# A first stage that interleaves the layer-0 product, the projection weights and the first tile's projections

## What is computed

```python
x = x + x @ w_eff.T                      # layer 0: w_eff from a codebook of 64 levels
...
q, k, v = x @ Wq.T, x @ Wk.T, x @ Wv.T   # layer 1: 32 query heads, 8 key heads, D = 128
q, k = rope(rmsnorm(q)), rope(rmsnorm(k))
k_all = concat(k_cache[block_table], k)  # 512 cached keys + 32 new ones per batch
probs = softmax(where(valid, q @ k_all.T * SCALE, -1e30))
x = x + (probs @ v_all) @ Wo.T
```

## Time and profile before

| | us |
|---|---|
| median of 3 runs | 2267.26 |
| lowest, highest | 2263.91, 2267.69 |
| profiled execution | 2268.09 |
| its span, first to last instruction | 2266.1 |

### The profile page before, as it was taken

How to read it: one execution, slowest core, us unless ns; L and a number is a source line. 1 busy time by engine, 2 the same in 40 slices (tenths; PEclk the granted TensorE clock), 3 DMA queues, 4 the chain that set the end, 5 groups by cost and what they waited for, 6 DMA issues and landing times.

```text
span 2266.1 us, 61278 instructions
## 1 busy us (share of the span) xinstructions
PE 2165.7 (96%) x18068; PEld 1417.1 (63%) x18068; DVE 1728.6 (76%) x3942; ACT 1470.7 (65%) x4967; POOL 1242.9 (55%) x2067
## 2 busy tenths in 40 slices
PE   5786779999999999999999999999999999999998
PEld 2343456666666666666666666666666666666665
DVE  6996458777787777777777777777777777777785
ACT  2542267777776767776667767777666666666674
POOL 3421026656655665555666666665665656656663
PEclk9997889999999999999999999999999999999999
DMA  3784666667667666666768768666666666566663
GB/s 102 225 282 165 216 221 202 191 204 204 195 195 216 204 199 205 204 197 198 208 186 259 207 184 253 176 176 179 190 180 178 176 180 188 177 178 177 183 180 99
DMA packets 472535, 438.32 MB, mean 193 GB/s; under 512 B 52861, under 2 KB 399308, under 8 KB 471694
## 3 DMA queue, kind: packets, MB, share of 16 engines
q1 hardware_dynamic: 427086, 295.96, 44.1%
q0 software_dynamic: 40960, 134.25, 19.3%
q10 hardware_dynamic: 4160, 4.19, 0.5%
HBM read 377.50 MB, written 56.70 MB: 192 GB/s over the span
## 4 chain that ended last, share of the span: by engine, by line
PE 83%; DVE 1%; issue 0%; ACT 0%; another core or an unknown queue 0%; DVEq 0%; ACTq 0%
PE PR L1058 21%; PE Op L1037 15%; PE WOp L1095 15%; PE Sp L1003 14%; PE PTp L1014 11%; PE TRp L1071 3%; PE Sp L1006 2%; PE Op L1019 1%; PE Op L1039 1%; PE TRp L1082 1%; DVE masked L1280 0%; DVE pts L1285 0%; DVE OT L1298 0%; DVE y L1335 0%; DVE masked L1291 0%
## 5 line engine op out<-in xcount | busy, mean ns | idle before, releaser
L778 POOL DMA_INDIRECT pages<-values_split,rows x512 | 516.0, 1008 | 194.4 <-issue 181.4
L1058 PE MATMUL PR<-Wt,xT 128*128 128x512 f16 x2304 | 557.0, 380 | 1.9 <-DVE Wt L1343 1.9
L1166 ACT ACTIVATE pts<-PTp 128x512 f16<-128x512 f32 x512 | 305.9, 597 | 357.9 <-PE PTp L1014 278.8
L1037 PEld LDWEIGHTS Op<-pts,pages 128*128 128x128 f16 x6144 | 384.9, 98 | 126.0 <-DVE OT L1298 8.1
L1037 PE MATMUL Op<-pts,pages 128*128 128x128 f16 x6144 | 426.7, 219 | 6.1 <-DVE OT L1298 5.2
L1280 DVE CUSTOM_DVE_ANT_0 masked<-Sp,mask 128x544 f32<-128x544 f32 x512 | 369.7, 722 | 81.9 <-PE Sp L1006 41.0
L1003 PE MATMUL Sp<-pages,qT 128*128 128x512 f16 x1536 | 415.7, 379 | 3.5 <-PEq L184 3.4
L1172 ACT ACTIVATE masked<-masked,small 128x544 f32<-128x544 f32 x512 | 379.9, 742 | 39.4 <-DVE small L1280 31.2
L1285 DVE TENSOR_TENSOR pts<-PTp,pts 128x512 f16<-128x512 f32 x512 | 351.1, 686 | 66.2 <-ACT pts L1166 47.2
L1095 PE MATMUL WOp<-WoT,OT 128*128 128x512 f16 x1536 | 377.5, 379 | 0.0
L1058 PEld LDWEIGHTS PR<-Wt,xT 128*128 128x128 f16 x2304 | 225.6, 98 | 196.3 <-issue 4.7
(11 more groups left out here) (202 smaller groups left out, 3047.9 us busy)
## 6 DMA issues: line engine op xcount, KB each, us to landing
pages<-keys_transposed SPq DMA_DIRECT2D x2048, 64.0 KB
mask<-mask_rows SPq DMA_DIRECT2D x128, 128.0 KB
v<-new_values SPq DMA_DIRECT2D x96, 128.0 KB
weights_split<-wdst SPq DMA_DIRECT2D x40, 256.0 KB
keys_transposed<-pages SPq DMA_DIRECT2D x32, 256.0 KB, 3.7
values_split<-pages SPq DMA_DIRECT2D x16, 512.0 KB, 3.9
xT<-x_transposed SPq DMA_DIRECT2D x32, 256.0 KB
rope_s<-rope_table SPq DMA_DIRECT2D x32, 256.0 KB
```

The costliest lines, as they stand in the source:

```text
L778: nc.gpsimd.indirect_dma_start(out=vS[:, n % 2, c, :, :].rearrange("p l n -> p (l n)"), out_offset=None, in_=v_d, in_offset=bass.IndirectO ...
L1037: nc.tensor.matmul(o, vS[:, par, c, low, h * D:(h + 1) * D], pts[:, u % 2, part, c * P:(c + 1) * P], start=(k == 0), stop=False)
L1058: m = nc.tensor.matmul(bank(k), xT[:, c, xl, :], Wp[:, c, wl, GROUP_COL[k]:GROUP_COL[k] + HID], start=(i == 0), stop=(i == NPASS - 1))
L1166: nc.scalar.activation(pts[:, u % 2, 0, :], PTp[:, :], ACT.Copy).then_inc(G.pt_hi, 1)
```

## The change

Blocks 3 and 4 become one, first_block, of 17 steps. Step t turns x of tile t + 1, turns two weight pieces (steps 0 to 11: the 24 pieces of the projections), makes half a group of tile 0's projections (steps 2 to 13), the product of tile t, and turns x1 of tile t - 1. The five banks for pieces become one (Op); the projections use PTp and WOp, the rotated heads half of Sp. Buffers move: weT and x into OT's space, the turned x1 into pts, x1 into masked. x1 of tile 0 is written straight into xT. The first four x tiles and the first weight group are loaded at the end of block 2, which waits for them. The 16 output pieces of the first half are turned in slots 1 to 16 of the loop (bank WOp, into WoT), and the 40 pieces of the second half start at slot 1 of tile 1. SP loads the pieces between parts of a batch of pages.

```diff
+OWN = QHH
 PIECES = (GROUPS + KVH) * 4
-PIECE_SLOTS = [UPT * t + sl for t in range(TILES - 2) for sl in (1, 8, 13)][1:PIECES + 1]
+PIECE_SLOTS = list(range(1, OWN + 1)) + [UPT * t + sl for t in range(1, TILES) for sl in (1, 8, 13)][:PIECES]
...
 FIRST_PLAN = dict(
-    proj={s: [(s // 2, NPASS // 2 * (s % 2), NPASS // 2 * (s % 2 + 1))] for s in range(12)},
-    squares={2 * k + 1: k for k in NORMED}, values=5, values_low=6,
-    root={2 * k + 1: k for k in NORMED}, scale={2 * k + 2: k for k in NORMED},
-    rope={2 * k + 2: k for k in NORMED}, add={2 * k + 3: k for k in NORMED},
-    turn={min(2 * k + 5, 14): k for k in NORMED}, turned={min(2 * k + 5, 14) + 1: k for k in NORMED}, wo={})
+    proj={2 * k + 2 + i: (k, i) for k in range(GROUPS) for i in range(2)},
+    squares={2 * k + 3: k for k in NORMED}, scale={2 * k + 4: k for k in NORMED},
+    rope={2 * k + 4: k for k in NORMED}, add={2 * k + 5: k for k in NORMED},
+    turn={2 * k + 5: k for k in NORMED}, turned={2 * k + 6: k for k in NORMED}, values=7)
...
+        xin = OTs[:, 4096:8192].bitcast(F32).rearrange("p (r n) -> p r n", r=4)
+        xTs = qT[:, 1, :, :].rearrange("p b c -> p (b c)")
+        xTa = [xTs[:, 1024 * i:1024 * (i + 1)].rearrange("p (c l n) -> p c l n", c=IC, l=2) for i in range(2)]
+        x1b = [masked[:, 0, 0:HID], masked[:, 1, 0:HID]]
...
+                sp.wait_ge(G.table_stored, 64)
+                for t in range(4):
+                    sp.dma_start(xin[:, t, :], x_d[t]).then_inc(G.x_first, 16)
+                sp.wait_ge(G.pages_stored, 32)
+                sp.dma_start(stage[0], weight_source(0, 0)).then_inc(G.stage_first, 16)
+                sp.wait_ge(G.x_first, 64)
+                sp.wait_ge(G.stage_first, 16)
...
         def load_piece(sp, p):
-            s, j = divmod(p, 4)
-            sp.dma_start(wsrc[:, p % 2, :].rearrange("p (c n) -> p c n", c=4), weight_source(1, s)[:, :, j * P:(j + 1) * P]).then_inc(wsrc_loaded[p % 2], 16)
+            half, q = (0, p + 4 * GROUPS) if p < OWN else (1, p - OWN)
+            sp.dma_start(wsrc[:, p % 2, :].rearrange("p (c n) -> p c n", c=4), weight_source(half, q // 4)[:, :, q % 4 * P:(q % 4 + 1) * P]).then_inc(wsrc_loaded[p % 2], 16)
...
+        def piece_bank(p):
+            return WOp[:, :] if p < OWN else TRp[:, :]
+        def piece_dest(p, part):
+            return WoT[:, p, part, :] if p < OWN else wdst[:, part, :]
...
+        def first_block():
...
+                    load_stage(sp, 0, 1)
+                    load_table(sp, 0)
+                    load_mask(sp, 0)
+                    load_mask(sp, 1)
+                    sp.wait_ge(G.numbers_loaded, 16)
+                    numbers = page_numbers(0)
+                    load_pages(sp, numbers, 0)
+                    for t in range(4, TPS + 5):
+                        if t < TPS + 4:
+                            sp.wait_ge(G.x1_done, t - 3)
+                        if t < TPS:
+                            sp.dma_start(xin[:, t % 4, :], x_d[t]).then_inc(x_loaded[t % 4], 16)
+                        if t < TPS + 4:
+                            sp.dma_start(out_d[t - 4], x1b[t % 2]).then_inc(x1_stored[t % 2], 16)
+                        if t >= 5:
+                            sp.wait_ge(G.xb_lo, t - 4)
+                            sp.dma_start(xT_d[t - 5], x_turned(t - 5).rearrange("p c l n -> p (c l n)")).then_inc(xT_stored[(t - 5) % 2], 16)
+                        if t in (5, 7, 9, 11):
+                            s = (t - 1) // 2
+                            sp.wait_ge(G.pe_done, 4 * (s - 1))
+                            load_stage(sp, 0, s)
+                        if t == 13:
+                            sp.wait_ge(G.vn_lo, 1)
+                            store_new_values(sp, 0)
+                        if t == 14:
+                            sp.wait_ge(G.vn_stored, 16)
+                            load_new_values(sp, 0)
+                        if t == 16:
+                            sp.wait_ge(G.pe_done, WPIECES)
+                            numbers = page_numbers(1)
+                            load_numbers(sp, 0)
+                        if 16 <= t < 20:
+                            load_pages(sp, numbers, 1, range(4 * (t - 16), 4 * (t - 16) + 4))
...
+                    def turn_weights(k):
+                        s, j = k // 4, k % 4
+                        if j == 0 and s >= 1:
+                            pe.wait_ge(stage_loaded[s % 2], 16 * (s // 2 + s % 2))
+                        if k >= 1:
+                            pe.wait_ge(G.evac_lo, k)
+                        for c in range(4):
+                            m = nc.tensor.transpose(Op[:, c * P:(c + 1) * P], stage[s % 2][:, j, c * P:(c + 1) * P], ident[:, :])
+                        m.then_inc(G.pe_done, 1)
...
+                    turn_x(0)
+                    for t in range(STEPS):
+                        first, second = pieces_of(t)
+                        if t + 1 < TPS:
+                            turn_x(t + 1)
+                        if first is not None:
+                            turn_weights(first)
+                        if t in plan["proj"]:
+                            k, part = plan["proj"][t]
+                            project(k, 6 * part, 6 * part + 3)
+                        if t < TPS:
+                            product(t, 0, 6)
+                        if second is not None:
+                            turn_weights(second)
+                        if t < TPS:
+                            product(t, 6, 12)
+                        if t >= 1:
+                            turn_x1(t - 1)
+                        if t in plan["proj"]:
+                            project(k, 6 * part + 3, 6 * part + 6)
+                        if t in plan["turn"]:
+                            turn_rotated(plan["turn"][t])
...
+                    lo_x(0)
+                    for t in range(STEPS):
+                        if t in plan["turned"]:
+                            rotated_low(plan["turned"][t])
+                        if t + 1 < TPS:
+                            lo_x(t + 1)
+                        for k in pieces_of(t):
+                            if k is not None:
+                                weights_low(k)
+                        if t < TPS:
+                            add_x(t)
+                        if t >= 1:
+                            lo_x1(t - 1)
+                        if t in plan["rope"]:
+                            rotate(plan["rope"][t])
+                        if t == plan["values"]:
+                            new_values_low()
...
+                            if own < OWN + 2:
+                                sp.wait_ge(G.w_turned, own - 1)
+                                load_piece(sp, own)
+                                own += 1
...
+                            for part in (range(0, 5), range(5, 10), range(10, NPP)):
+                                load_pages(sp, numbers, batch % KBUFS, part)
+                                if own < OWN + 2 and (past >= 0 or own < 4):
+                                    sp.wait_ge(G.w_turned, own - 1)
+                                    load_piece(sp, own)
+                                    own += 1
...
+                        if first == 0 and ti == 1:
+                            pe.wait_ge(G.w_lo, OWN)
...
-        tile_block([1], proj=[0], prep=True)
-        tile_block([t % 2 for t in range(ALL_TILES)], attn=True, proj=range(ALL_TILES - 1), wo=range(1, ALL_TILES + 1))
+        first_block()
+        tile_block([t % 2 for t in range(ALL_TILES)], proj=range(ALL_TILES - 1), wo=range(1, ALL_TILES + 1))
```

More of the change, by code:

```diff
@@ L771, in build @@
-        clear()
         def gather(n, c):
@@ L988, in _ @@
+                    for buf in range(KBUFS):
+                        sp.wait_ge(k_loaded[buf], 16 * NPP * sum(n % KBUFS == buf for n in range(2, NB)))
+                    store_y(len(wo) - 2)
+                    load_y(len(wo) - 1)
+                    store_y(len(wo) - 1)
+                    sp.wait_ge(G.y_stored, 16 * len(wo))
                 @block.tensor
@@ L1074, in turn_piece @@
                     def turn_piece(p):
-                        turns = turns_before(PIECE_SLOTS[p])
+                        turns = turns_before(PIECE_SLOTS[p]) if p >= OWN else 0
                         pe.wait_ge(wsrc_loaded[p % 2], 16 * (p // 2 + 1))
@@ L1368, in _ @@
                             residual(ti - 1)
-                        if attn and s >= 2:
+                        if s >= 2:
                             probs_low(s - 2)
```

703 lines of the change are left out of this document (358 added, 345 removed).

## The result

| | before | after |
|---|---|---|
| median, us | 2267.10 | 2244.28 |
| lowest to highest | 2263.91 to 2267.69 (4 runs) | 2243.66 to 2245.12 (4 runs) |
| profiled execution | 2268.09 | 2244.90 |
| its span | 2266.1 | 2243.0 |

What follows compares the result with a forecast made beforehand. The long loop was taken as TensorE-bound at full clock, with savings possible only in the first 337 us. 2268.1 minus 32.0 (loop start 304.5 against 336.52) plus 9.2 lost in the loop gives 2245.3, stated as 2245; range 2236 to 2258.

Steps and rivals of the forecast that it cites:

- cold clock: Merged stage's start: the same two turns and product run at low clock as before, costing 4.3 us.
- waits: Merged stage: turns of weight pieces wait for the single bank Op, 0.4 us a step, 5 us in all.
- Content: Merged stage: PE's full-clock work, products and x turns 54.9, weight pieces 10.4, projections 15.6, turned heads 1.7, together 82.6 us.
- DMA: Merged stage: the x wait at 236.39 should go; loads coming together at the start put at 0, bounds 0 and 7 us.
- Start: Merged stage: a weight wait replaces the x wait; last load lands at 202.8, PE starts at 204.2.
- End: Last product to loop: as before, 8.36 us, with the last pages landing under that.
- Loop: 16 more turned groups in tile 0, 7.0 us, plus 2.2 for slots where VectorE is behind: loss 9.2 us.
- Rival 1: First loop tile paced by VectorE or by the pieces' loads: loss 17 instead of 9, 2253 us; chance 0.2.
- Rival 2: Merged stage paced by its copies or starved at the start: waits of 11, late load of 7, 2258 us; chance 0.12.
- Rival 3: No waits at all in the merged stage, and tile 0 hides a part: 2237 us; chance 0.1.
- rival 4: Short waits for Op keep TensorE at low clock in merged steps 0 to 11: +61, 2307 us, slower; chance 0.04.
- Rival 5: Transpositions in the merged stage fall to the low clock level, 61 groups at 0.43 us more: +26, 2271 us; chance 0.02.

Runs made afterwards that it cites:

- run 3: Changed kernel with the product cut 8 and 4 matmuls instead of 6 and 6 around the second weight piece's turn: 2240.65 us, ratio 0.9891.
- Run 4: Kernel before the change, its two 1 MB weight loads asked for at steps 5 and 10 of the product stage instead of both at step 8: 2261.25 us.
- Run 9: Changed kernel with the first weight group and four x tiles asked for ahead of both last key stores of the threshold stage: 2240.74 us, ratio 0.9891.
- run 6: Changed kernel with the second batch's page loads at steps 15 to 18 instead of 16 to 19: 2243.35 us, ratio 0.9904.
- run 11: The changed kernel itself timed again, in the same rounds as run 12: 2242.84 us, ratio 0.9898 to the kernel before.
- run 1: Changed kernel without the 16 output pieces in tile 0; the first half's output weights stay zero, that part of the result left out: 2238.03 us, ratio 0.988.
- run 7: Changed kernel with matmuls whose result nobody reads, filling PE's gaps late in the threshold stage and at the merged stage's end: 2245.43 us, ratio 0.9911.
- run 8: Changed kernel with the edits of run 3, run 5, run 6 and run 7 together: 2237.37 us, ratio 0.9876.
- run 12: The kernel of run 10 plus 18 matmuls whose result nobody reads at the merged stage's end: 2235.36 us, ratio 0.9864 to the kernel before.
- Run 2: Changed kernel with weight pieces, projections and rotations moved 16 steps later, behind all products of the same block: 2274.58 us, ratio 1.0041.
- run 10: Changed kernel with the edits of run 3, run 6 and Run 9 together, without added matmuls: 2236.13 us, ratio 0.9872.
- run 5: Changed kernel with the first weight group and four x tiles asked for ahead of the last key store of the threshold stage: 2241.27 us, ratio 0.9894.

## Why the prediction was right
Its steps against the profile after, first in the order of the sum:

| term | forecast | measured |
|---|---|---|
| first turn of the merged stage | 204.2 | 204.83 |
| PE's work, cold clock and waits, to the last product's end | 82.6 + 4.3 + 5 = 91.9 | 296.70 - 204.83 = 91.87 |
| end, last product to loop | 8.36 | 9.60 |
| loop start | 304.5 | 306.30 |
| loss in the loop, tiles 0, 1, 13 and 14 | 9.2 | 8.55 |
| loss from the loop's start to the end of the span | 9.2 | 7.1 |
| profiled execution | 2245.3 | 2244.9 |

- **The last row is partly luck.** The gain ahead of the loop was 30.2 us, not 32.0; the loss from there to the end of the span was 7.1, not 9.2. Two errors of about 2 us against each other leave 0.4. Of the second, 1.4 us is the last tile, which was long in the profiled execution of the kernel before and has nothing to do with the change.
- **Content, cold clock and waits.** The sum of the three came out to 0.03 us, with the cold stretch 0.7 us longer and the waits 0.7 us shorter than forecast. The cold stretch is 9.30 us (204.83 to 214.13) for work that takes 4.33 at full clock (3.46, and two pieces of 0.43), so 5.0 instead of 4.3; what is left over the work of 82.6 and the cold 5.0 is 4.3 us of waits instead of 5. The listed ones are 2.7, and seven times the 0.22 that each costs above its bracket make 1.5: 4.2. They are those that were named, for VectorE's copy out of Op: with the cover moved (run 3) they are gone from the list, and 2.1 us with them.
- **DMA, put at nothing.** No wait for an x tile or a weight group stands in the stage. Run 4 shows that the old wait of 4.71 us came with the two loads of 1 MB at once; asked for apart, they leave one of 1.19.
- **Start.** The weight load took the place of the x load's wait, as forecast, 0.6 us later. Run 9 shows that it was the moved loads and not the meeting of the engines.
- **End, the term that was mis-sized.** I wrote "as before, 8.36 us" and that the last pages "land under that". They do land, but their issue takes SP 1.92 us, and it stands ahead of the last store. That is 1.0 of the 1.24 us (run 6); the end of the change's other profile (run 11) was 9.23, so some 0.4 vary by themselves. Costing a transfer by its landing and not by its time on the issuing queue was the error.
- **Loop.** The 7.0 us for 16 turned groups was right: in run 1, whose slot 0 is as long as the change's, a piece comes to 0.49 us (7.34 over 15). The 2.2 us for slots in which VectorE is behind was right in sum and not in kind. Slots 11 to 14 hide part of a turn (they grew by 0.38, 0.20, 0.13 and 0.30), slot 6, with a rotation, grew by 0.77; but these nearly cancel. What fills the place of the 2.2 is the clock: slots 0 and 1 are 1.8 us longer, of which one turn explains 0.43. The other 1.4 differ between executions of the same kernel (run 11).
- **Rivals 1 and 2.** Tile 0 took 60.6, not 68, and steps 2 to 11 took 5.6 to 6.6, not 7. In tile 0 PE's waits for VectorE are single ones under 1 us, and none for a load is listed. Rival 1's second half is not far off, though: with the added matmuls (runs 7, 8 and 12) pieces' loads do come late, by 0.39 to 1.25 us.
- **Rival 3** did not come true, though a cut of the product that leaves fewer waits exists (run 3).
- **Rivals 4 and 5.** After the waits of 0.23 to 0.54 us the clock stayed at 1.00 through all the windows from 215 us on, and the groups of four transpositions from 214 us on took 0.60 to 0.66 us, as in the earlier trace rows. Run 2 shows the other case: with a wait of mostly 0.77 us in every 2.07, the clock did fall after 35 us at full rate. The Trainium skill (TensorE: Matmul & The Clock Gate, Part 4: PE-mode transpose) says that the full rate does not engage for transpositions; the windows after, with four or five such groups in every step of 6 us at a clock of 1.00, contradict it for this kernel, where matmuls of 512 columns stand between them.
- **Its working.** The 65.8 us in rival 4 add up to 65.4, and 16 x 0.43 to 6.9, not 7.0; neither moves the forecast.

The expectations of the variants were less good than the forecast. Those that priced work and waits from PE's and SP's own rows held (runs 1, 3, 6, 9 and 10, though in 3 and 9 the parts less well than the sum); those that rested on where SP would be held up, or on what the clock would do, missed (5, 7, 8, 12). Run 4 gave about 5 of the 6.6 us. Run 2 missed by 5 us, not in the chain through the bank but in the heads' wait for GpSimd behind it.

## What to carry to other kernels
When a stage is a chain through one bank, its cost is not PE's work but turn, copy and subtraction in a row; it becomes nearly free once more than two microseconds of other PE work stand between two links (here 2.4 us left no listed wait, 1.95 left up to 0.39, and 0.65 mostly 0.77). So with one bank, merge stages only if their instructions are really interleaved, and count the work between two uses of a bank when placing the filler. Price a DMA twice: when it lands, and how long it keeps the issuing queue from what stands behind it, above all ahead of the last store before a meeting of all engines. Look at the wait of a stage's first instruction: what it waits for can often be asked for during the stage before, but only ahead of the waits that the issuing queue will stand in.

## What the hardware showed that I had not expected
- **The low-clock stretch at a stage's start varies by itself.** From the first to the fourth turn of x, the change took 14.14 and 14.15 us in its two profiled executions, and variants with the very same steps took 12.68 to 13.83 (runs 1, 5, 6 and 9; those of 5 and 9 had other loads in flight). In the loop, the first two slots took 8.18 and 6.67 us in the same two executions of the change. So of a gain of a microsecond at such a place one profile tells nothing.
- **Idle time ahead of the loop, and its first slot:** 1.59 us gave 2.44 (full clock), 3.37 gave 3.90, 6.50 gave 3.79, 6.86 gave 4.72. A short gap kept the clock; beyond that (run 2: 2.76 gave 3.89) the length of the gap does not order the cost.
- **The clock also fell behind shorter gaps.** In run 8 a gap of 2.07 us left the clock full, and it fell in the next one of 1.41, 0.63 us of PE's work later. In run 2 it fell among waits of under 1 us, with PE at work for 1.08 of every 2.07 us.
- **Sixteen page loads of 64 KB keep SP's queue for 8 to 9 us** (four take 1.90 to 2.15, sixteen in one go 9.16), against 0.38 to 0.95 for a load of 1 MB: it is the number of issues that fills the queue, not the bytes.
